# Moving the weight splits of a mixture-of-experts stage behind the hidden-layer split

## What is computed

```
logits = silu(t @ rw1 + rb1) @ rw2 + rb2          # 8 experts per token
vals, idx = top_k(logits, 2)                       # 2 of them used
w  = softmax(masked logits)
eh = silu(einsum('td,edh->teh', t, ew1) + eb1)     # 1024 -> 256
eo = einsum('teh,ehd->ted', eh, ew2) + eb2         # 256 -> 1024
y  = t + einsum('te,ted->td', w, eo)
```

## Time and profile before

| | us |
|---|---|
| median of 3 runs | 1152.09 (1144.93 to 1162.6) |
| the profiled execution's own time | 1144.93 |
| its span | 1143.2 |
| expert stage, first hidden matmul to last matmul of the last step | 926.6 to 1126.4 |
| last instruction after it (landing of the scatters) | to 1143.2 |

### The profile page before, as it was taken

One profiled execution on the slowest core, in us unless ns is written; L12 is line 12 of the kernel. 1 busy time (PEld: TensorE's weight loads), 2 busy tenths in 40 slices (PEclk: granted clock), 3 DMA queues, 4 the chain that ended last, 5 costly groups with the idle time before them and its releaser, 6 DMA issues.

```text
span 1143.2 us, 17965 instructions
## 1 busy us (share of the span) xinstructions
PE 1056.7 (92%) x6444; PEld 1009.1 (88%) x6444; DVE 624.1 (55%) x1109; ACT 439.8 (38%) x932; POOL 161.2 (14%) x166
## 2 busy tenths in 40 slices
PE   2699999999998999999999999999999469999994
PEld 1599999999998999999999999999999459999993
DVE  5738888888835254234422432264222467878872
ACT  5644445354411122212112111165322247777762
POOL 2000000000000002000200020002443123453432
PEclk9999999999999999999999999999999769999997
DMA  5503322233123662004300340176565078999975
GB/s 131 145 1 105 106 77 59 76 105 104 50 89 110 204 189 73 1 1 130 97 1 1 129 121 1 37 229 188 175 180 186 8 286 268 316 329 304 320 188 92
DMA packets 72793, 148.86 MB, mean 130 GB/s; under 512 B 11866, under 2 KB 50711, under 8 KB 68209
## 3 DMA queue, kind: packets, MB, share of 16 engines
q1 hardware_dynamic: 61117, 112.34, 30.4%
q0 software_dynamic: 10976, 34.65, 12.3%
q10 hardware_dynamic: 596, 0.48, 0.1%
HBM read 108.40 MB, written 42.96 MB: 132 GB/s over the span
## 4 chain that ended last, share of the span: by engine, by line
PE 88%; DVE 5%; issue 3%; ACT 1%; DMA 1%; DVEq 1%; POOLq 0%; POOL 0%; PEld 0%; ACTq 0%
PE ps L1389 20%; PE ps L871 14%; PE ps L1461 10%; PE ps L2019 9%; PE ps L1120 8%; PE ps L1428 8%; PE ps L2036 6%; PE ps L737 4%; PE ps L675 3%; PE ps L2005 2%; PE ps L659 1%; PE ps L1447 1%; PE ps L833 1%; DVE key_hot L730 1%; ACT xn L645 1%
## 5 line engine op out<-in xcount | busy, mean ns | idle before, releaser
L1351 POOL TENSOR_TENSOR s_rows<-s_rows,b1t 125x1368 f32<-125x1368 f32 (+3 forms) x9 | 23.9, 2669 | 626.1 <-DMA s_rows<-in_x 626.1
L744 DVE TENSOR_TENSOR adj<-ps,adj 125x250 f32 x212 | 88.2, 416 | 43.3 <-PE ps L737 35.4
L871 PE MATMUL ps<-h_lo,w_hi 128*128 128x418 f32 x336 | 108.5, 371 | 0.0
L871 PE MATMUL ps<-h_hi,w_hi 128*128 128x418 f32 x336 | 100.3, 379 | 0.0
L1428 PE MATMUL ps<-z_hi,adj 125*125 125x342 f32 (+1 forms) x300 | 95.0, 322 | 1.6 <-DVE s_rows L1660 1.6
L1428 PE MATMUL ps<-z_lo,adj 125*125 125x342 f32 (+1 forms) x300 | 94.3, 319 | 2.3 <-issue 2.3
L871 PE MATMUL ps<-h_hi,w_lo 128*128 128x418 f32 x336 | 93.4, 359 | 0.0
L2104 DVE TENSOR_TENSOR w_lo<-w_raw,w_hi 128x2048 fp32r<-128x2048 f32 x34 | 77.8, 2289 | 28.5 <-ACT w_hi L2061 21.9
L1120 PE MATMUL ps<-adj,y_hi 125*128 125x416 f32 (+1 forms) x240 | 86.7, 361 | 3.4 <-issue 3.4
L1120 PE MATMUL ps<-adj,y_lo 125*128 125x416 f32 (+1 forms) x240 | 86.4, 360 | 0.3 <-issue 0.3
L737 PE MATMUL ps<-key_hot,src_hot 125*125 125x250 bf16 x424 | 80.8, 271 | 3.8 <-DVE adj L744 3.3
(11 more groups left out here) (295 smaller groups left out, 2645.8 us busy)
## 6 DMA issues: line engine op xcount, KB each, us to landing
w_raw<-in_L_ffn_ew SPq DMA_DIRECT2D x34, 1024.0 KB, 8.4
xin<-in_x SPq DMA_DIRECT2D x10, 448.0 KB
t_d<-xn SPq DMA_DIRECT2D x10, 448.0 KB
base<-x_d POOLq DMA_DIRECT2D x10, 448.0 KB, 4.1
out<-base POOLq DMA_DIRECT2D x10, 448.0 KB, 3.4
y_d<-y_hi SPq DMA_DIRECT2D x7, 625.0 KB
y_d<-y_lo SPq DMA_DIRECT2D x7, 625.0 KB
self_d<-self SPq DMA_DIRECT2D x7, 625.0 KB
```

What stands on the lines that cost most here:

```text
L744: e.tensor_tensor(cols, ps[0:P, 5 + b % 2, 0:KW].rearrange("p (t w) -> p t w", t=NT), cols, ALU.add).then_inc(self.took, 1)
L871: mm = e.matmul(BANK(m, own, c), wt[:, own, k, :], ht[:, k, a:a + w], start=(k == 0 and p == 0), stop=(k == KT - 1 and p == 2))
```

## The change

On ACT, `w1(s+1)` and `w2(s)` move from their places ahead of and inside the loop over j to the end of `head(s)`, behind hid_hi. On DVE, the two weight splits (`w(0, ...)` of s+1 and `w(1, ...)` of s) move likewise behind hid_lo, and the four xt_lo groups stand together ahead of it. Nothing is added or removed, and SP, POOL and PE keep their order.

```
             def head(s, u, q):                                  # scalar
                 x = e.value_load(step_x[0:1, ds(ORDER[s], 1)], min_val=0, max_val=NX - 1)
-                if more(s):
-                    w1(s + 1, 1 - u, q + u)
                 for j in range(HK):
                     wait_apart(e, m_g1, HK * s + j + 1 + 4)
                     e.activation(hid[:, u, j, 0:WIDE(s)], ps[:, 2 + j, 0:WIDE(s)], ACT.Silu, bias=...).then_inc(m_h, 1)
                     if more(s):
                         rows(s + 1, 1 - u, q + u, range(2 * j, 2 * j + 2))
-                    if j == 0:
-                        w2(s, u, q)
                 e.wait_ge(m_h, HK * s + HK + 2)
                 e.wait_ge(m_g2, GROUP_AT(s - 1) + 2 * NB)
                 e.activation(hid_hi[:, u, :, 0:WIDE(s)], hid[:, u, :, 0:WIDE(s)], ACT.Copy).then_inc(m_hhi, 1)
+                if more(s):
+                    w1(s + 1, 1 - u, q + u)
+                w2(s, u, q)
...
             def head(s, u, q):                                  # vector
                 if more(s):
-                    w(0, w1_raw, w1_hi, w1_lo, s + 1, 1 - u, q + u)
-                    rows(s + 1, 1 - u, q + u, range(0, 2))
-                w(1, w2_raw, w2_hi, w2_lo, s, u, q)
-                if more(s):
-                    rows(s + 1, 1 - u, q + u, range(2, 4))
+                    rows(s + 1, 1 - u, q + u)
                 e.wait_ge(m_hhi, s + 1)
                 e.tensor_tensor(hid_lo[:, u, :, 0:WIDE(s)], hid[:, u, :, 0:WIDE(s)], ...).then_inc(m_hlo, 1)
+                if more(s):
+                    w(0, w1_raw, w1_hi, w1_lo, s + 1, 1 - u, q + u)
+                w(1, w2_raw, w2_hi, w2_lo, s, u, q)
```

## The result

The changed kernel takes 1184.79 us (median of 4 runs, 1183.34 to 1189.29), the kernel before 1155.27 (4 runs, 1144.93 to 1162.6). The ratio is 1.0292 (95% interval 1.021 to 1.0377): slower, by some 30 us where 1176 us and a range of 1163 to 1190 had been forecast. The direction and the range held.

The account below looks back on a forecast made before the run. PE was taken to bound the kernel. Waits and a later end (23.3 us), clock drops (3.4) and step 0 (0.8) sum to 27.5 us: 1172.4 on own time, 1179.6 on the median; 1176 forecast, range 1163 to 1190.

Parts of the forecast that it names:

- The place and the length of the holes: PE waiting for w1_lo: 3.02 us in six heads behind small steps, 2.3 more at head(1), 0.29 in four other steps.
- The cover: Later additions on DVE leave about one microsecond before PE waits for xt_lo or freed banks; claimed to cost nothing.
- The end: In step 16 the w2 split stands ahead of tail(15)'s additions, delaying the last scatter: 1.7 us more.
- The clock term: Half clock behind PE's holes: two drops of 1.7 us each (bounds none to six), plus 0.8 us at step 0.
- The case with all six drops: Five or six clock drops and a long low stretch at step 0: 35.4 us more, 1187.5 on the median; 15 in 100.
- The baseline: Profiled execution of 1144.93 us, fastest of three, against their median of 1152.09; the forecast took a value between.
- The rival on the other side: Scatters, not PE, set the end and hide PE's holes; only 1.7 us paid, 1153.8; 3 in 100.
- The page's rule on the clock: Only idle gaps beyond a certain length halve PE's clock; all six holes are under it, leaving 23.3 us plus step 0.

Follow-up runs that it names:

- e1: Kernel before with only the w1 split moved behind hid_hi and hid_lo, w2 split left in place: 1188.08 us, ratio 1.0275.
- e2: Kernel before with only the w2 split moved, w1 staying ahead of the first half: 1154.04 us, ratio 1.0045.
- e4: Kernel before with the change made only in the ten steps whose step before is big: 1162.38 us, ratio 1.0095.
- e11: Changed kernel with scatters of only the first 512 values of each row, second half of the output left out: 1173.67 us, ratio 1.0245.
- e5: Changed kernel with steps 4 and 12, whose holes stand ahead of small heads, kept in the old order: 1174.2 us, ratio 1.0233.
- e6: Changed kernel with steps 6 and 9, whose holes stand ahead of big heads, kept in the old order: 1181.18 us, ratio 1.0289.
- e12: Kernel before, unchanged, run once more with a profile: 1161.69 us.
- e7: Kernel before with all four xt_lo groups ahead of the w2 split in step 0 alone: 1155.26 us, ratio 1.0063.
- e10: Kernel before with scatters of only the first 512 values of each row, second half of the output left out: 1142.42 us.
- e9: Kernel before with POOL's order turned, the gather of each turn ahead of the scatter: 1173.65 us, ratio 1.0228.
- e3: Changed kernel with 20 never-read matmuls ahead of PE's w1_lo wait in head(1) and the six heads with holes: 1175.63 us, ratio 1.0178.
- e8: Kernel before with xt_lo moved in step 0 and never-read matmuls added around head(0) and head(1): 1158.01 us, ratio 1.0123.

## Why the prediction was right, and where it was not

- **The place and the length of the holes: right.** PE waits for w1_lo in the six heads behind a small step and in head(1). Start to start they cost 6.15 - 3.26 = 2.89 us (forecast 3.02), head(1) 2.2 (forecast 2.3), the four steps with a long tail and a small step next 0.18 (forecast 0.29). e1 shows that it is w1, and the six holes are 2.72 or 2.73 us in every kernel that has them (5.11 to 5.17 at head(1)).
- **The cover: right for the change, thin as said.** In the changed kernel PE waits for o_rows only once, 0.4 us, and never in mid-stage for xt_lo. e2 and e4 used the cover up with one more split ahead of xt_lo and paid 0.3 to 1.6 us a time.
- **The end: 1.7 forecast, 3.0 measured,** from the last matmul on, and 0.4 in the last tail. The path that the working took, the w2 split ahead of the additions of tail(15), delays the scatter behind them by 1.65 us (additions done at 1170.09 against 1122.27, both counted from the last matmul at 1172.56 and 1126.39). It left out a second path: both splits of step 15 delay the additions of tail(14) and so the scatter of step 14, whose landing came last and held the scatter of step 15 for 1.2 us more. The last bias write waited 2.8 us for POOL by the same landing.
- **The clock term failed in size.** It was 1.7 us for each of two holes and 0.8 at step 0, 4.2 together. In the profiled execution it was 18.8 from head(1) on and 3.1 ahead of it, which is not shown to belong to the change; from head(1) on it was 21.9 in e1's and 9.5 in e11's. Two steps of the working were wrong: five of six holes were followed by low clock, not two, and the low stretch behind a hole was taken to last as long as the one seen at 940 (3.4 us), while it lasted up to 17 us, above all ahead of small heads (e5 against e6). The case with all six drops had been given 15 in 100 and 35.4 us; by its mechanism it was the one that came. The trace of before had a warning against reading the fall from the length of idle gaps alone. At 373.9 the clock fell with no gap at all, shortly behind 2.34 us in which PE did only twenty matmuls of 1x1; the working counted two falls in this trace and left this third one out:

```profile
370.68 2.34 PE L1168 MATMUL ps<-ones,dinv_row 1*125 1x1 f32 x20
```

```profile
373.90:377.30 3.40, 3.40 (x12) 0.50 0.94 287
```

- **The baseline hid the error.** The sum was made against an execution (1144.93) that had no late gathers. The median of before has them: three sets of its runs have medians of 1158.5, 1152.58 and 1151.61, and e12 and e7 show where the 7 to 17 us over the undisturbed time lie. The changed kernel's scatters wait for DVE (109.4 us, 14 times) and hardly for landings (15.4, 3 times), and none of the profiles with its six holes shows a late gather. So against an undisturbed execution of before the change costs about 40 to 45 us (e1's profiled 1188.45 against 1144.93 is 43.5), and in the medians some 10 us of that are covered by losses which only the kernel before has. That is argued from profiles and from e10; e11, which should have widened the difference to 36 to 42 us, gave 31 in the median and 39 in those of its runs that have the changed kernel's clock, so how much is covered is open. That the forecast of 1176 lies within 9 us of 1184.79 is thus in part luck: a clock term some 15 us too small in the profiled execution, against a baseline that loses time in a way the changed kernel does not.
- **The rival on the other side** (the scatters lead the end) fell: PE's holes were paid in full, and in mid-stage POOL's scatters waited for DVE. But at the very end its sign is there, a scatter that waits for a landing (1172.09; the table of waits puts its 6.4 us down to DVE, whose additions were done before the landing), and its ground was real: in many executions the chain of scatters holds up the kernel before.
- **The page's rule on the clock**, that it takes long idle gaps (the Trainium skill, "TensorE: Matmul & The Clock Gate", section "HAM oscillation — how this bites in real kernels"), does not hold here: 2.72 us sufficed five times in six, and 1.41 us did in e9. The measurement decides.

## What to carry to other kernels

When a producer is moved back in its engine's queue, compare for every kind of step the time from a common event to the product with the time from it to the consumer; the shortest piece of cover work (here the tail of a small step) decides, and only those steps pay. A hole in TensorE's queue then costs more than its length because of the low clock behind it: here on average one and a half times as much ahead of 256-wide matmuls (2.9 + 1.3 us) and nearly three times ahead of 128-wide ones (2.9 + 5.3), with a wide spread between executions of one order (e1, e11). And look at more than one execution of the kernel before: an own time at the low edge of its runs is a different baseline from their median.

## What the runs showed of the hardware that had not been expected

- A busy TensorE can stay at its low level: 17.0 us of 17.0 busy at clock 0.50 behind the hole at 1110.28, 13.4 of 13.4 in e3 and 16.82 of 16.9 in e8, each beginning with the 128-wide matmuls of a small step; in these three it rose only when wider matmuls had begun. It is not always so: in head(0) of the kernel before it rose at 933.7 in the midst of the same 128-wide work.
- Filling the idle time with matmuls kept the clock at 1.00 at all four big heads, and not at the two small ones (e3).
- The landing time of a scatter, not its issue, sets how early the gather behind it in POOL's queue starts (e12: a scatter that had waited 9.9 us for a landing, and a gather 7.1 us late behind it). Halving the scatters took 9 us from the median and nearly two thirds of the spread (e10).
